# A decoder layer with top-2 experts: the last six batches routed in one group in place of a group of four and one of two

## What is computed

```
g = gelu(xt @ wg1 + bg1); probs = softmax(g @ wg2)
top_vals, top_idx = top_k(probs, 2)
gates = zeros.at[n, top_idx].set(top_vals)
h = gelu(xt @ w_in[e]);  o = h @ w_out[e]
y = sum over e of gates[n, e] * o[e]
x = layernorm(x + y)
```

## Time and profile before

| what | us |
|---|---|
| three runs | 425.79 (median), 424.82, 425.82 |
| profiled execution, its own time | 424.05 |
| its span from first to last instruction | 422.3 |
| TensorE busy | 344.7 (82%) |
| VectorE busy | 308.2 (73%) |
| ScalarE busy | 221.9 (53%) |
| GpSimd busy | 218.0 (52%) |
| mean granted clock of TensorE | 0.93 of full |

### The profile page before, as it was taken

The page is one execution under the profiler, slowest core; times in us unless marked ns, Lnnn a source line. Parts: engine busy times, 40 slices in busy tenths (PEclk is TensorE's granted clock), DMA queues, the critical chain, the costliest instruction groups (busy, mean ns, idle before and its releaser), DMA issues. The chain is left out here.

```text
span 422.3 us, 12354 instructions
## 1 busy us (share of the span) xinstructions
PE 344.7 (82%) x4025; PEld 279.1 (66%) x4025; DVE 308.2 (73%) x912; ACT 221.9 (53%) x518; POOL 218.0 (52%) x287
## 2 busy tenths in 40 slices
PE   2977999999999999999888664688999999999100
PEld 1656777877778687776766343576899999988100
DVE  2866989888888888888887737378777655655193
ACT  3425666676766766667765236263545444343044
POOL 8344456765757657576547762633223333422173
PEclk9998999999999999999999885589999999999755
DMA  7610222210222112220012221416434322221493
GB/s 223 223 36 1 78 76 77 76 57 23 77 76 79 40 39 76 78 77 23 32 52 75 81 78 47 157 52 191 142 104 127 90 75 68 88 64 40 148 362 125
DMA packets 21387, 38.35 MB, mean 91 GB/s; under 512 B 3696, under 2 KB 11120, under 8 KB 21328
## 3 DMA queue, kind: packets, MB, share of 16 engines
q1 hardware_dynamic: 16768, 26.06, 19.7%
q0 software_dynamic: 3408, 9.41, 6.2%
q10 hardware_dynamic: 1152, 2.10, 1.3%
HBM read 24.71 MB, written 12.84 MB: 89 GB/s over the span
## 5 line engine op out<-in xcount | busy, mean ns | idle before, releaser
L586 POOL DMA_INDIRECT parts<-QKT,rows_all x39 | 37.6, 964 | 76.8 <-DVE QKT L1220 70.4
L328 PE MATMUL bank<-QS,EW 128*128 128x256 f16 (+1 forms) x384 | 61.7, 262 | 4.0 <-DVE XB L1033 2.6
L492 POOL TENSOR_TENSOR rstd<-veps,neghalf 128x1 f32<-128x1 f32 x48 | 38.7, 806 | 38.5 <-DVE veps L856 38.1
L1396 PE MATMUL bank<-EW,QV 128*128 x312 | 48.6, 273 | 1.4 <-DVE R L1212 0.5
L1212 DVE TENSOR_TENSOR R<-scratch,QV 128x512 f16<-128x512 f32 x39 | 26.8, 691 | 30.1 <-ACT scratch L776 18.4
L328 PE MATMUL bank<-XB,EW 128*128 128x256 f16 (+1 forms) x192 | 48.5, 261 | 0.0
L776 ACT ACTIVATE scratch<-bank 128x512 f32<-128x512 f32 x39 | 23.4, 600 | 39.2 <-PE bank L328 39.1
L328 PEld LDWEIGHTS bank<-QS,EW 128*128 x384 | 37.4, 101 | 10.0 <-issue 4.7
L1138 DVE TENSOR_REDUCE NM<-bank 128x4 bf16<-128x512 f32 x64 | 39.6, 679 | 2.8 <-PE bank L1551 2.5
L507 POOL DMA_INDIRECT bkt<-REC,dest x32 | 31.7, 989 | 18.5 <-DVE REC L898 8.6
L710 ACT ACTIVATE rows_all<-bank 128x512 f32<-128x512 f32 x64 | 33.2, 604 | 13.7 <-remote 6.9
(11 more groups left out here) (240 smaller groups left out, 938.4 us busy)
## 6 DMA issues: line engine op xcount, KB each, us to landing
scratch<-w_in SPq DMA_DIRECT2D x8, 512.0 KB, 3.8
scratch<-w_out SPq DMA_DIRECT2D x8, 512.0 KB, 3.3
rows_all<-bkt SPq DMA_DIRECT2D x15, 262.0 KB
XC<-x SPq DMA_DIRECT2D x16, 128.0 KB, 3.5
XC<-ctx SPq DMA_DIRECT2D x16, 128.0 KB, 3.3
EW<-parts SPq DMA_DIRECT2D x8, 256.0 KB, 6.7
EW<-parts ACTq DMA_DIRECT2D x8, 256.0 KB, 8.1
out<-rows_all SPq DMA_DIRECT2D x8, 256.0 KB, 2.1
```

What stands on the lines that cost most here:

```text
L328: last = pe.matmul(dst, a(c), b(c), start=(c == 0 and i == 0), stop=(c == n - 1 and i == 2))
L492: pool.tensor_tensor(rstd[n][p][:], veps[n][p][:], neghalf[:, 0:1], ALU.pow).then_inc(s_rs[n], 1)
L586: pool.indirect_dma_start(parts, bass.IndirectOffsetOnAxis(ap=home[:, t, f:f + 1], axis=0), Y[t % 2][:, f, :], None).then_inc(s_put[t % 2] ...
L1396: last = pe.matmul(bank[4 + t % 2][:, f * D:(f + 1) * D], a[t % 2][:, h, f * P:(f + 1) * P], b[:, h, :], start=(h == 0 and i == 0 and f == 0),
```

## The change

`EDGE` loses the bound 14, so that batches 10 to 15 are one group. `NG` becomes 2, and everything that depends on it follows: `s_rec_ok`, `s_dest` and `s_scat` of group 1 now cover 12 scatters in place of 8 (and 4 for group 2). The bank lists lose their third entry. The three tail strings are rewritten: one `gelu`, `lg`, `exps`, `choice`, `gate`, `dest`, `cnt` in place of two of each, no `cntpre:2`; on VectorE `full:2` and `full:3` stand ahead of `choice1:1`, and `full:2` also ahead of `n2:15`; on TensorE `turn:0` stands ahead of `lg:1`, with `upa:0` between `lg:1` and `cnt:1`. GpSimd's and SyncE's orders are unchanged.

```diff
-EDGE = (0, EARLY, 14, NB)
+EDGE = (0, EARLY, NB)
 NG = len(EDGE) - 1
...
-        LGP = [bank[(7, 5, 5)[g]][:, 0:(EDGE[g + 1] - EDGE[g]) * NE] for g in range(NG)]
-        PLP = [bank[(6, 4, 4)[g]][:, 256:256 + (EDGE[g + 1] - EDGE[g] + 1) * NE] for g in range(NG)]
+        LGP = [bank[(7, 5)[g]][:, 0:(EDGE[g + 1] - EDGE[g]) * NE] for g in range(NG)]
+        PLP = [bank[(6, 4)[g]][:, 256:256 + (EDGE[g + 1] - EDGE[g] + 1) * NE] for g in range(NG)]
...
ScalarE:
-                     "X2T:13 lns:15 rec:15 gcp:13 gelu:1 X2T:14 exps:1 X2T:15 second:1 gcp:15 gelu:2 high:0 "
-                     "exps:2 second:2 high:1")
+                     "X2T:13 lns:15 rec:15 gcp:13 X2T:14 X2T:15 gcp:15 gelu:1 high:0 "
+                     "exps:1 second:1 high:1")
...
VectorE:
-                     "mx3:15 R2:13 s2:13 ewl:15 O2T:14 nr:14 n2:13 ewl:16 R2:14 s2:14 O2T:15 nr:15 full:1 R2:15 s2:15 n2:14 "
-                     "choice1:1 n2:15 choice2:1 full:2 gate1:1 dest:1 gate2:1 full:3 "
-                     "choice1:2 low:0 choice2:2 whose:0 gate1:2 dest:2 gate2:2 low:1 whose:1")
+                     "mx3:15 R2:13 s2:13 ewl:15 O2T:14 nr:14 n2:13 ewl:16 R2:14 s2:14 O2T:15 nr:15 full:1 R2:15 s2:15 n2:14 full:2 n2:15 full:3 "
+                     "choice1:1 low:0 choice2:1 whose:0 gate1:1 dest:1 gate2:1 low:1 whose:1")
...
TensorE:
-                     "cntpre:1 gh:13 ao2:15 lg:1 x2T:14 x2T:15 gh:15 cnt:1 cntpre:2 lg:2 turn:0 upa:0 cnt:2 turn:1 upb:0")
+                     "cntpre:1 gh:13 ao2:15 x2T:14 x2T:15 gh:15 turn:0 lg:1 upa:0 cnt:1 turn:1 upb:0")
```

## The result

| | before | after |
|---|---|---|
| median (lowest to highest), us | 425.81 (424.82 to 426.77) | 433.86 (429.27 to 434.95) |
| ratio, 95% interval | | 1.0179 [1.0142, 1.0216] |
| profiled execution, span, us | 424.05, 422.3 | 434.95, 432.1 |
| mean granted clock | 0.93 | 0.92 |

One group in place of two costs 8.05 us by the medians. The forecast was +5.0, with a range of +2 to +8.8. In one experiment, edge12, seven of ten runs, the profiled one among them, lie more than 1.5% above the fastest of that kernel, and its ratio rests on the other three. Past L1200 a line of after has a number one lower than in before.

A forecast was written before the change was run, and what follows sets the result against it. The tile stage was taken as bound by TensorE, its start set by tile 3's load. Later scatters +3.4 and clock +1.6 gave +5.0 us on the median 425.79: 430.8 us, range 427.8 to 434.6, chance 0.60.

The forecast's parts named there:

- The count's signal: At cnt:1, before dest:1: VectorE gets the signal with 0 extra delay, no scatters running beside it; 3.8 us kept for the range.
- Rival (b): At the counts: signal late as before without scatters beside it, dest:1 onward 3.8 us later; +8.8 us, 434.6; chance 0.10.
- Rival (c): In the scatter burst: VectorE holds each of 8 added scatters by one operation; +5.5 us more, 436.3; chance 0.03.
- (d): Chain to tile 3 shorter: turn, lg:1 and upa:0 run at full clock; 426.7 us, no change; chance 0.07.
- (e): Ahead of turn 3: TensorE's signals come promptly and scatters don't bind; -3.0 us, 422.8; chance 0.06.
- the release of tile 3's load: Ahead of turn 3: release passes from the tables at 286.0 to the last of twelve scatters at 289.4; +3.4 us.
- rival (a): Ahead of tile 3: burst holds up TensorE's signals, idle too short for a clock drop; +3.4 us, 429.2; chance 0.14.
- the clock: After the idle stretch ahead of turn 3: TensorE works at half the clock for 3.1 us; +1.6 us.

The follow-up runs named there:

- edge12: Kernel before with group bound 12 in place of 14 (groups of 10, 2 and 4 batches): median 428.97 us beside 426.58, ratio 0.9975.
- pause_late: Kernel before with a short GpSimd pause after every second scatter of groups 1 and 2: 428.02 us, ratio 1.0038.
- hold: Changed kernel, with the first of the twelve scatters waiting until up 1 of TensorE has signalled: 436.11 us, ratio 1.0215 to the kernel before.
- pause_burst: Changed kernel with a short pause (one pow of 128 x 1) after every second scatter of the twelve: 437.02 us, ratio 1.0267 to the kernel before.
- twice: Kernel before with every put of the tile stage issued a second time, into a spare DRAM array: 474.8 us, ratio 1.1121.
- three_in_a_row: Kernel before with 24 further puts, for the first half of each tile only: 442.69 us, ratio 1.0395.
- full_alone: Kernel before with only full:2 ahead of n2:15 on VectorE and X2T:15 ahead of exps:1 on ScalarE, groups unchanged: 429.2 us, ratio 1.0086.
- twice_hw: Kernel before with 39 plain stores of the puts' size from ScalarE's queue, without GpSimd: 427.1 us, ratio 1.0031.

## Why the prediction was right, and where not

**Right.** The sign, the stretch, and a size inside the range. Counted from scatter 19 the chain went as worked out:

| step, us after scatter 19 | predicted | measured |
|---|---|---|
| turn 0 starts | 6.5 | 6.4 |
| upa:0 starts | 11.6 | 11.1 |
| counts end | 14.5 | 14.1 |
| gate2:1 ends | 15.8 | 15.5 |
| last scatter in | 33.0 | 32.8 |
| turn 3 starts | 36.5 | 39.0 |

The gelu of three pairs cost nothing, the new lg:1 took 1.30 us (I had 1.5), choice1 1.65 (1.6), the pitch was 13.91 / 11 = 1.265 us. **The count's signal**: VectorE went on 0.11 us after the recorded end of the counts (274.64), with no scatter beside it. Rival (b) is refuted as put, and the 0 that I took in place of 3.8 was right for the reason given, as pause_late shows too. Rival (c) falls with the pitch, (d) and (e) with the sign.

**Wrong, the release of tile 3's load.** The step was "the release of tile 3's load passes from the tables at 286.0 to the scatters at 289.4". It passed back: the base was ready 2.7 us after the last scatter was in. The error stands in the next paragraph: "upb, turn 2, up 1, down 0, up 2 and down 1 should run with less idle ... They would be done between 285 and 287. This gains nothing". That is 28.6 to 30.6 us after scatter 19; down 1 ended 39.0 us after it. I had seen that a burst of scatters might hold a signal, and used it for cnt:1, where it is absent; I did not use it for up 1 to down 1, all of which now run beside a burst of twelve. I had that thought only in rival (a), as a cause for a shorter idle, not for a later end: its mechanism came nearest to what happened, and its sum of +3.4 lacks the same term. The scatters alone give turn 3 at 293.4 + 3.5 = 296.9; it came at 299.62, **2.7 us for the hold**. Hold and pause_burst show that it is the hold and not VectorE's order: with up 1 freed the base is ready 10 us sooner, counted from scatter 19. No run puts the tables ahead of the low half in the changed kernel; by after's trace that alone would not bring turn 3 forward, since down 1 ended only just before it.

**Wrong, the clock.** The +1.6 us were put behind turn 3. Turn 3 ran at full clock (0.66 us for four, as in the earlier trace rows), and from turn 3 to the end of the span it took 132.5 us, against 132.8 before. The low clock came, from 286.6 to 296.8, but mostly while TensorE was held and issued one or two matmuls at a time. Of its dense work only the 2.9 us of up 2 from 293.9 to 296.8 ran at 0.50, which is 1.5 us lost ahead of turn 3, whose rows could not have come sooner either.

**Luck in the number.** The sum by what was measured is 3.4 + 2.7 = 6.1, counted from scatter 19 against the profile of before (39.0 - 33.1 = 5.9). But that profile was also slow behind its scatter 19: its base of tile 3 came 29.6 us after it, 28.0 and 27.9 us in twice and three_in_a_row. By these the release moves from 28.0 to 32.8, which is 4.8 us, and with the hold it is 4.8 + 2.7 = 7.5; the turns say 39.04 - 31.46 = 7.6 and the medians 8.05. So my +5.0 was near because errors partly cancel: 1.6 us that were not there, and 2.7 and 1.4 us that I had not counted. Why the profile of before has this stretch longer is open; no run was made for it.

**What stays open** is how the hold works. The runs show what sets it off (the length of the row: nothing beside three, delays of 1 to 3 us beside four, 6 to 8 beside eight, 8 to 11 beside twelve, 15 beside fourteen), what doesn't (the bytes of the DMA engines, the mean rate of GpSimd's DMAs) and what ends or prevents it (the landing of the row's last DMA; a pause of 1.4 us after every second one; in full_alone, one case, 0.7 us was not enough). They do not show whether GpSimd's issuing or its transfers are the cause. Whether the matmuls themselves run late or only their signals and the following issues do, the profile can't tell: its matmul ends are modelled.

## What to carry to other kernels

When work is merged so that one engine's DMAs go out in one unbroken row, look not only at when the last one lands but at what every other engine does meanwhile: a short row split in two by the wait for a second group was worth more here than the steps it saved. A recorded matmul end is no proof that its consumer could start; look for "remote" waits of ScalarE and VectorE that end when the last DMA of GpSimd's row lands. An edit that was meant to set the length of a row has to be read back from the trace: three_in_a_row did not keep it, and its total alone would have led to the wrong rule. And a part of a change that brings its own stage forward (full_alone: about 1 us at turn 0) can still lose, if it closes a gap that another engine lived by.

## What the runs showed of the hardware that was not expected

- Rows of four or more of GpSimd's indirect DMAs 1.26 us apart hold TensorE. With twelve, up 1 came through 11.4 us after its recorded end (14.8 for up 2 in hold, with fourteen); with eight 7.9 us (edge12); with puts in rows of four to eight the whole kernel lost 11% (twice). Eleven rows of three cost nothing (three_in_a_row). The Trainium skill, SBUF — State Buffer, section Who interferes with whom, says that "PE and ACT never wait on anyone". Of SBUF ports that may hold, and no run here looks at ports; as a rule for planning which work can lie beside GpSimd's DMAs these runs speak against it.
- The bytes of the added puts of twice, stored from a hardware queue, cost 1.5 us, 0.3%, for 39 stores (twice_hw).
- SyncE too seems to be slowed in such a row: 2.7 us from the landing of the last scatter to the issue of the load in hold, where two puts stood behind the scatters, against 0.7 us from the base to the load in before. One case, not tested.
